# Weights of small diagonal blocks added to the scores as logarithms on TensorE

## The reference

```
delta  = query - key
mask   = -log(delta + 1) for delta > 0,  0 for delta = 0,  -inf for delta < 0
scores = q k^T / sqrt(8) + mask
out    = softmax(scores) v
```

## Time and profile before

| | |
|---|---|
| median of 3 runs | 627.3 us (626.72 to 627.9) |
| profiled execution | 626.35 us |
| its span, first to last instruction | 624.5 us |
| TensorE busy, matmuls | 564.4 us, 90% |
| VectorE busy | 562.8 us, 90% |
| GpSimd busy | 537.4 us, 86% |
| ScalarE busy | 400.8 us, 64% |
| TensorE weight loads | 250.9 us, 40% |
| mean granted TensorE clock | 0.985 |

### The profile page before, as it was taken

The page is one execution under the profiler, slowest core; times in us unless marked ns, Lnnn a source line. Parts: engine busy times, 40 slices in busy tenths (PEclk is TensorE's granted clock), DMA queues, the critical chain, the costliest instruction groups (busy, mean ns, idle before and its releaser), DMA issues.

```text
span 624.5 us, 11270 instructions
## 1 busy us (share of the span) xinstructions
PE 564.4 (90%) x3807; PEld 250.9 (40%) x3807; DVE 562.8 (90%) x1178; ACT 400.8 (64%) x857; POOL 537.4 (86%) x400
## 2 busy tenths in 40 slices
PE   6999779999999999999989899999989898989985
PEld 5576534444343334333333332342334242432322
DVE  6899998989999999999999999998989999997661
ACT  4576457566656475767667577666656667759782
POOL 7226987789899989999998999999998999998992
PEclk9999988999999999999999999999999999999997
DMA  5255341310000000200000000000000000000000
GB/s 148 74 137 114 119 83 51 78 43 36 2 2 3 0 2 10 86 1 2 2 0 2 19 1 1 2 2 1 1 2 1 19 0 2 1 2 1 1 2 17
DMA packets 14715, 16.66 MB, mean 27 GB/s; under 512 B 1594, under 2 KB 14171, under 8 KB 14243
## 3 DMA queue, kind: packets, MB, share of 16 engines
q1 hardware_dynamic: 14123, 15.70, 9.2%
q10 hardware_dynamic: 536, 0.26, 0.2%
HBM read 11.75 MB, written 4.01 MB: 25 GB/s over the span
## 4 chain that ended last, share of the span: by engine, by line
PE 43%; POOL 32%; DVE 13%; ACT 7%; issue 4%; ACTq 0%; POOLq 0%; DVEq 0%
POOL ring L802 25%; PE psum L1396 11%; PE psum L1354 9%; PE psum L1378 7%; DVE mxp L1135 7%; ACT ring L954 2%; POOL xw L820 2%; POOL xw L818 2%; PE psum L1331 2%; POOL xw L822 2%; PE psum L1312 2%; PE psum L1314 1%; PE psum L1320 1%; DVE ring L1162 1%; PE psum L1404 1%
## 5 line engine op out<-in xcount | busy, mean ns | idle before, releaser
L802 POOL TENSOR_TENSOR ring<-ring,dist 128x1024 f32<-128x1024 f32 (+3 forms) x223 | 438.4, 1996 | 31.7 <-ACT ring L954 31.3
L1135 DVE TENSOR_REDUCE mxp<-psum 128x1 f32<-128x512 f32 (+3 forms) x640 | 352.6, 598 | 20.5 <-PE psum L1354 11.4
L954 ACT ACTIVATE ring<-psum 128x512 f32<-128x512 f32 (+3 forms) x446 | 211.5, 528 | 101.5 <-PE psum L1381 51.9
L1354 PE MATMUL psum<-kop,qop 96*128 96x512 bf16 (+3 forms) x640 | 198.0, 352 | 7.3 <-DVE mxp L1135 5.3
L1378 PE MATMUL psum<-qop,kop 128*128 128x512 bf16 (+3 forms) x640 | 190.7, 349 | 6.2 <-DVE mxp L1135 3.7
L1396 PE MATMUL psum<-ring,vaug 128*32 128x512 f32 (+3 forms) x1280 | 151.5, 544 | 15.0 <-POOL ring L802 14.1
L1162 DVE TENSOR_TENSOR ring<-psum,dist 128x512 f32<-128x512 f32 (+3 forms) x194 | 115.7, 622 | 13.9 <-ACT psum L954 13.8
L954 ACT ACTIVATE psum<-psum 128x512 f32<-128x512 f32 (+3 forms) x194 | 99.5, 543 | 39.7 <-PE psum L1378 23.4
L1354 PEld LDWEIGHTS psum<-kop,qop 96*128 96x128 bf16 x640 | 57.2, 97 | 127.8 <-DVE mxp L1135 46.5
L1378 PEld LDWEIGHTS psum<-qop,kop 128*128 128x128 bf16 x640 | 59.7, 97 | 82.2 <-DVE mxp L1135 15.5
L1357 PE MATMUL psum<-tri_q,identb 128*128 128x128 bf16 x256 | 56.2, 221 | 0.0
(11 more groups left out here) (130 smaller groups left out, 490.2 us busy)
## 6 DMA issues: line engine op xcount, KB each, us to landing
kop<-parts_dram SPq DMA_DIRECT2D x9, 384.0 KB
qop<-parts_dram SPq DMA_DIRECT2D x9, 384.0 KB
parts_dram<-qpart SPq DMA_DIRECT2D x18, 128.0 KB, 2.8
xin<-_attn_hidden_states_dram SPq DMA_DIRECT2D x4, 256.0 KB, 4.7
ring<-inv_dram SPq DMA_DIRECT2D x1, 1024.0 KB, 4.9
out_dram<-xin SPq DMA_DIRECT2D x4, 256.0 KB, 2.3
parts_dram<-qpart SPq DMA_DIRECT2D x6, 96.0 KB
qop<-parts_dram SPq DMA_DIRECT2D x3, 192.0 KB
```

Of the source, the lines that this page charges most:

```text
L802: g_.tensor_tensor(slot(p)[:, :, 0:n], slot(p)[:, :, 0:n], both, ALU.mult).then_inc(weighed_pool, 1)
L954: a_.activation(scores if pair_vec[p] else slot(p)[:, e % 2, 0:n], scores, ACT.Exp, scale=SCALE).then_inc(exp_done, 1)
L1135: v_.tensor_reduce(mxp[:, u % 2, 4 * a + j, c - g:c - g + 1], bank(*o)[:, 0:n], AX_X, ALU.max).then_inc(max_used, 1)
L1354: ins = mm(bank(*o)[:, 0:n], qop[0:K_MAX, u // NQ % 2, h, P * a:P * (a + 1)], kop[0:K_MAX, h, k0:k0 + n], start=True, stop=(c != g))
```

## The change

For the small pairs, those with d of 0, 1 or 2 (`LOG_D`), there is a third way of weighing. When TensorE is given the first head's scores and GpSimd's planned queue is over `LOG_QUEUE` = 3000 ns, the pair is marked (`pair_vec` is None), and neither GpSimd nor VectorE weighs it. Instead TensorE adds sqrt(8) times the logarithm of the weights to the scores, ahead of the exponential: three products of the identity with the three bfloat16 parts of this matrix, of all of the head's queries. The triangle's mask is contained in the first part, so the product with `tri_k` goes. ScalarE's exponential then gives the weighed value directly, to the ring. The product with the values waits for the pair's exponentials.

The logarithms are made once, after `dist`: on ScalarE the logarithm, its scaling and the first part, on GpSimd the rest, on ScalarE the second part, on GpSimd the third and the addition of the triangle to the first. They cover the last 384 columns of `dist`. The condition for marking includes that this is done, by the planner's clock.

To make room, `flip` and the buffer of the logarithms lie in slots of the ring that are idle then, and the maxima of the 4-bit blocks (`amax`) have one small tile for all six pieces.

```diff
@@ plan()
+    act(("log", 0), LW, [("ACT", ("dist", NG - 1))], n=3, rank=3)
+    pool(("log", 0), 1050, [("ACT", ("log", 0)), ("POOL", ("consts",))], rank=0)
+    act(("log", 1), LW, [("POOL", ("log", 0))], rank=3)
+    pool(("log", 1), 1400, [("ACT", ("log", 1))], rank=0)
@@ take()
+        if engine == "PE" and kind == "st":
+            u, b = steps[item[1] // 4]
+            d = b - TPG * units[u][0]
+            if (item[1] % 2 == 0 and d < LOG_D and ("POOL", ("log", 1)) in seen
+                    and max(clock["POOL"], now) + waiting["POOL"] - now > LOG_QUEUE):
+                pair_vec[item[1] // 2] = None
+            if pair_vec.get(item[1] // 2, False) is None:
+                more = (PARTS * P * (d + 1) - P) * PE_COL
+                took, end = took + more, end + more
         if engine == "ACT" and kind == "st":
...
-            if e % 2 == 0:
+            by_pe = pair_vec.get(p, False) is None
+            if e % 2 == 0 and not by_pe:
...
-            if pair_vec[p]:
+            if by_pe:
+                weighed_by[e] = "ACT"
+                seen[("ACT", ("weigh", e))] = end
+            elif pair_vec[p]:
@@ buffers
-        flip = sb("flip", [P, P], F32)
-        amax = sb("amax", [P, NB], F32)
+        amax = sb("amax", [P, WHALF // BLK], F32)
+        flip = ring_flat[:, 5632:5632 + P]
+        logw = sb("logw", [P, PARTS, LW], BF16)
+        logs = ring_flat[:, 6144:6144 + LW]
@@ GpSimd
+                if o[0] == "log":
+                    if o[1] == 0:
+                        pool.wait_ge(log_part1, 1)
+                        g_.tensor_tensor(logs, logs, logw[:, 0], ALU.subtract).then_inc(log_rest1, 1)
+                    else:
+                        pool.wait_ge(log_part2, 1)
+                        g_.tensor_tensor(logw[:, 2], logs, logw[:, 1], ALU.subtract).then_inc(log_ready, 1)
+                        pool.wait_ge(consts_ready, 5)
+                        pool.wait_ge(log_rest1, 1)
+                        g_.tensor_tensor(logw[:, 0, LW - P:LW], logw[:, 0, LW - P:LW], tri_k[:],
+                                         ALU.add).then_inc(log_ready, 1)
@@ ScalarE
+                if o[0] == "log":
+                    if o[1] == 0:
+                        act.wait_ge(dist_ready, NG)
+                        a_.activation(logs, dist[:, S - LW:S], ACT.Ln).then_inc(log_seq, 1)
+                        act.wait_ge(log_seq, 1)
+                        a_.activation(logs, logs, ACT.Identity, scale=1.0 / SCALE).then_inc(log_seq, 1)
+                        act.wait_ge(log_seq, 2)
+                        a_.activation(logw[:, 0], logs, ACT.Identity).then_inc(log_part1, 1)
+                    else:
+                        act.wait_ge(log_rest1, 1)
+                        a_.activation(logw[:, 1], logs, ACT.Identity).then_inc(log_part2, 1)
@@ TensorE, scores
-                    if d < TPG:
+                    if pair_vec[e // 2] is None:
+                        pe.wait_ge(log_ready, 2)
+                        for i in range(PARTS):
+                            ins = mm(bank(*o)[:, 0:n], identb[:], logw[:, i, LW - n:LW],
+                                     start=False, stop=(i == PARTS - 1))
+                    elif d < TPG:
@@ TensorE, product with the values
+                    if None in pair_vec[2 * s:2 * s + 2]:
+                        pe.wait_ge(exp_done, 4 * s + 4)
```

More of the change, by code:

```diff
@@ L62 @@
 MROWS = 3
+LOG_D = 3
+LOG_QUEUE = 3000
+LW = P * LOG_D
 FILL = 200
@@ L520, in build @@
         dist_psum = sem("dist_psum")
+        log_seq = sem("log_seq")
+        log_part1 = sem("log_part1")
+        log_rest1 = sem("log_rest1")
+        log_part2 = sem("log_part2")
+        log_ready = sem("log_ready")
         dist_ready = sem("dist_ready")
@@ L751, in _ @@
             g_.memset(tri_k[:], 0.0).then_inc(pool_seq, 1)
-            g_.memset(flip[:], 0.0).then_inc(pool_seq, 1)
+            g_.memset(flip, 0.0).then_inc(pool_seq, 1)
             g_.memset(mxp[:].rearrange("p a b c -> p (a b c)"), NEG).then_inc(pool_seq, 1)
             pool.wait_ge(pool_seq, 7)
-            g_.affine_select(out=flip[:], in_=flip[:], compare_op=ALU.not_equal, fill=1.0, base=1 - P,
+            g_.affine_select(out=flip, in_=flip, compare_op=ALU.not_equal, fill=1.0, base=1 - P,
                              pattern=[[1, P]], channel_multiplier=1).then_inc(consts_ready, 1)
@@ L1034, in fp4_scale @@
                 v, c, of = xw[:, x0:x0 + w], qx[:, 0:w], slice(x0 // BLK, (x0 + w) // BLK)
+                most = amax[:, 0:w // BLK]
                 blocks = v.rearrange("p (a b) -> p a b", b=BLK)
@@ L1040, in fp4_scale @@
                         vec.wait_ge(xnT_psum, X_PIECES.index(n) + 1)
-                    ins = v_.tensor_reduce(amax[:, of], blocks, AX_X, ALU.max, apply_absolute_value=True)
+                    ins = v_.tensor_reduce(most, blocks, AX_X, ALU.max, apply_absolute_value=True)
                 else:
@@ L1044, in fp4_scale @@
                 if k == 1:
-                    ins = v_.tensor_scalar(sc[:, of], amax[:, of], 1.0 / 6.0, 1e-12, ALU.mult, ALU.max)
+                    ins = v_.tensor_scalar(sc[:, of], most, 1.0 / 6.0, 1e-12, ALU.mult, ALU.max)
                 if k == 2:
-                    ins = v_.reciprocal(amax[:, of], sc[:, of])
+                    ins = v_.reciprocal(most, sc[:, of])
                 if k == 3:
                     ins = v_.scalar_tensor_tensor(out=blocks, in0=blocks, scalar=BELOW_TIE,
-                                                  in1=spread(amax[:, of], w // BLK, BLK), op0=ALU.mult, op1=ALU.mult)
+                                                  in1=spread(most, w // BLK, BLK), op0=ALU.mult, op1=ALU.mult)
                 if k == 4:
@@ L1282, in _ @@
                     bank_free(*o)
-                    mm(bank(*o), flip[:], hankel[:, GQ * k:GQ * (k + 1)],
+                    mm(bank(*o), flip, hankel[:, GQ * k:GQ * (k + 1)],
                        start=True, stop=True).then_inc(dist_psum, 1)
```

## The result

The changed kernel takes 635.8 us (median of 4 runs, 634.68 to 636.4) against 627.0 us: ratio 1.0135, 95% interval 1.0122 to 1.0148. By the ratio it is slower by 8.5 us, where 10.5 us faster was forecast. Its profiled execution has a span of 632.9 us, against 624.5 us before.

A forecast was written before the change was run, and what follows sets the result against it. VectorE and GpSimd were taken to bound the kernel together, TensorE having room. From 626.35 us, minus 11.5 relief, plus 1.0 start, gives 615.85; with 0.95 for the median, 616.8 us. Range 604 to 634 us.

The forecast's parts named there:

- VectorE and GpSimd bound the kernel together, and TensorE follows with room: From 100 to 575 us: VectorE 95% and GpSimd 94% busy are the bound; TensorE's 93% overstates its load.
- The relief, 21.6 us, of which 11.5 arrives: Weighing taken off GpSimd (32.5 us) and VectorE (15.3), evened out to 21.6 us each; 11.5 us shortens the run.
- The count: Small pairs on the diagonal group that change hands: 40 of 96, bounds 20 and 96.
- 4.6 full pairs moved to GpSimd: Planner's evening out: each full pair moved takes 1.36 us off VectorE and puts 2.362 us on GpSimd.
- The "half": Share of the 21.6 us relief taken to arrive, 11.5 us, between all of it and none.
- What hides the 25 us is the 57 us that TensorE waits: TensorE's added products, 25.3 us, fit into its weight loads' 57 us of waits for VectorE's maxima.
- Weight loads of the products: On TensorE, 128-wide loads hidden under matmuls: nothing; if exposed, 16 us, kept for the range.
- The start, 1 us: Making logarithms on ScalarE takes 2.0 to 4.6 us, mostly hidden: 1 us, between 0 and 4.6.
- GpSimd's first weighing: Sign of being wrong at the start: this coming several us later than 60.52 us.
- The new order: Planner's dealing after the change: relief comes in lumps at ends of units, so only about half was taken to arrive.
- Rival 4: Slower: TensorE becomes the bound at the ends of units, in six small pairs in a row; +8, so 635 us; chance 0.20.
- VectorE's wait for scores: Sign: hardly longer if the forecast is right, grown by ten or more if wrong; 11.1 and 7.4 us before.

The follow-up runs named there:

- the old order: The planner's order of the kernel before with the items of the logarithms added; with logarithms made and no pair marked, 628.65 us, 1.0016.
- the exchange in the old order: Kernel before's order with logarithms made, the same 28 pairs' weighing struck and three products in its place, nothing dealt anew: 631.97 us, 1.0070.

## Why the prediction was wrong

- *VectorE and GpSimd bound the kernel together, and TensorE follows with room.* Wrong, and the first step that failed. 94 and 95% busy was read as being the bound. Striking 85 us from GpSimd gave a tenth of it back, almost none of it between the ends of units 1 and 10, and striking 21 us from VectorE 0.7 us; the waits took most of the rest. GpSimd's queue is a cushion: the planner gives it work whenever it is short of some, so it is full by construction, and VectorE likewise. The profile's page on the kernel before had a warning, its chain of work that ended last, where TensorE has the largest share and VectorE 13%:

```profile
PE 43%; POOL 32%; DVE 13%; ACT 7%; issue 4%; ACTq 0%; POOLq 0%; DVEq 0%
```

- *The relief, 21.6 us, of which 11.5 arrives.* The count was 28 pairs, not 40. GpSimd's total fell by 21.4 us and VectorE's by 11.3. That the first meets the 21.6 is luck: the sum had more pairs and 4.6 full pairs moved to GpSimd, while in fact four moved away from it (152 to 148, VectorE's heads 144 to 152). What the relief brought in the old order was 4.6 us, most of it in the first 115 us and part of that perhaps clock. The "half" had no row under it.
- *What hides the 25 us is the 57 us that TensorE waits.* Wrong, and the term with the largest price: the columns had the size worked out (28 pairs, 19.5 us), but cost 8.3 us instead of nothing. The waits of the weight loads were summed over the run, and were taken as room: with the products that sum fell only from 56.7 to 53.6 us, while 19.5 us were added. The columns cost in every stretch of the run, and did so too when spread evenly.
- *Weight loads of the products: nothing.* Three products of 384 columns stand in 0.65 us (at 67.32), the last one's 0.33 included, so they start at the rate of their columns. Right.
- *The start, 1 us.* 1.0 us measured. There is one more table load, where none or two were foreseen, and the scores of the first marked pair come 15 us after the logarithms. GpSimd's first weighing came at 63.66 us instead of 60.52, which was named as a sign of being wrong; with nothing marked it came at 62.25. Right in the size.
- *The new order* was only counted as a share of the relief not arriving. It costs 0.65%, 4.1 us, with the products in both orders, and 1.14% without them. VectorE being freed of weighing, the planner dealt maxima earlier, one of them before its operand had landed, and TensorE's queue is in order. This was missing from the rivals, though the planner's fixed 17 us for such a DMA stood in the code; how much of the 4.1 us that stall is stays open.
- *Rival 4, TensorE as the bound at the ends of units, 635 us*, hit the time with the right engine. Its place is not borne out, since lumps elsewhere and spread columns cost too, and VectorE's wait for scores, its sign, hardly grew in the changed kernel (18.5 to 18.9 us). In the old order it did grow with the products. The range stopped at 634, in the middle of this rival.

The sum by the runs: +1.0 start, -4.6 relief, +8.3 products, +4.1 order, 8.8 against 8.5 measured. The last term is itself the difference to the changed kernel, so what this sum tests is only that the first three add up to the exchange in the old order (4.7 against 4.4). What stays open is which chain closes the loop between the four queues in mid run. Less work on GpSimd or on VectorE shortens nothing between units 1 and 10, more columns on TensorE lengthen every stretch, and fewer shorten it a little where the clock stays up; that points at TensorE, but no run held its clock while columns were taken off.

## What to carry to other kernels

Where a planner deals work between engines, all of them look full, and none need be the bound: strike the work that is to be moved and look if the time falls, before paying for the move. A total of waits is not room: here the engine with 57 us of them still passed on some four tenths of the time of the columns added, even of those spread evenly. Look also at the clock of each run before putting a small difference down to the work that was moved. And when an order is dealt anew, look for operands that the new order needs sooner than their DMA lands.

## What the runs showed of the hardware

The warm-up of TensorE, 30 transposes from the same start, took 4.92 us in one execution and 6.43 in the other. Before:

```profile
5.69 4.92 PE L1196 MATMUL psum<-identf 128*128 128x128 f32 x30 [5.69 <-POOL identb L739]
```

After:

```profile
5.68 6.43 PE L1246 MATMUL psum<-identf 128*128 128x128 f32 x30 [5.68 <-POOL identb L766]
```

The code there is the same, and in the profiled executions of the other eighteen kernels it took between 4.82 and 6.34 us. TensorE starts six to eight transposes a microsecond at first and eleven or twelve later, from 9 us on in the one execution and from 12 us on in the other. The doubling suggests the clock's two levels, but the column of the granted clock shows 1.00 throughout, so that is not shown. VectorE's first maximum follows at 27.32 and 28.81 us, so up to 1.5 us of the 8.4 between the two profiled spans come from this and not from the change; the medians are over executions with different starts.

A table load on ScalarE took 1.28 us and the activation followed at once, in the changed kernel:

```profile
39.70 1.28 ACT L942 ACT_TABLE_LOAD   x1
40.99 0.52 ACT L942 ACTIVATE ring<-dist 128x384 f32<-128x384 f32 x1
```

ScalarE's previous activation had ended at 39.68 us, so no drain shows on either side. The 2.66 us a switch of the Trainium skill (ScalarE: Activation LUTs, What ACT_TABLE_LOAD costs) are not borne out here. In its section Table sets: the hidden batching unit, the Trainium skill counts one load for a logarithm followed by an exponential, since one set has both. Here the first exponential after the logarithm loaded a table again, at 51.52 us. The same section has the hyperbolic tangent in a set with the exponential, and the trace agrees: the tangents later loaded none. The prediction, which put the tangent in another set than the logarithm, left this out.
